# Narrow attention on four row strips, single-pass scores in the first and third wide attention, and a beginning in another order

## What is computed

```python
x = L0(ctx, x)   # attention of the tokens over (context, tokens), 16 heads of 16; MLP
x = L1(x, ctx)   # two wide cross-attentions (16 heads of 128, 64 keys + a bias key); MLP
x = L2(x, ctx)   # narrow cross-attention, 16 heads of 16, 64 keys, mask; MLP
x = L3(x, ctx)   # as L1
# wide:   weights = softmax((norm(x) @ wq + bq) . (ctx @ wk + bk, bias_k) / sqrt(128))
#         x += (weights @ (ctx @ wv + bv, bias_v)) @ wo + bo
# narrow: scores = where(mask, q . k * 16**-0.5, min);  x += softmax(scores) @ v @ cproj + b
# MLP:    x += gelu(norm(x) @ w1 + b1) @ w2 + b2
```

## Time and profile before

| | us |
|---|---|
| median of 3 runs | 928.24 (927.35 to 928.96) |
| profiled execution, its time | 924.61 |
| profiled execution, its span | 922.8 |
| PE busy | 859.1 (93%) |
| DVE busy | 630.1 (68%) |
| POOL busy | 550.4 (60%) |
| ACT busy | 496.9 (54%) |

### The profile page before, as it was taken

How to read it: one execution, slowest core, us unless ns; L and a number is a source line. 1 busy time by engine, 2 the same in 40 slices (tenths; PEclk the granted TensorE clock), 3 DMA queues, 4 the chain that set the end, 5 groups by cost and what they waited for, 6 DMA issues and landing times.

```text
span 922.8 us, 16592 instructions
## 1 busy us (share of the span) xinstructions
PE 859.1 (93%) x5936; PEld 711.8 (77%) x5936; DVE 630.1 (68%) x1329; ACT 496.9 (54%) x1204; POOL 550.4 (60%) x638
## 2 busy tenths in 40 slices
PE   4899977899999999999899898999999999999898
PEld 3677756899966799666798686899966699766798
DVE  3678886518889768897432499418889768898330
ACT  2677767555753357533563344755753357533562
POOL 2678884577943469564295053577853369564393
PEclk8899999999999999999999999999999999999999
DMA  6843212002550025200001100202550024100001
GB/s 192 278 125 104 92 40 104 1 1 92 163 215 1 1 69 171 104 1 1 6 19 36 57 1 1 104 1 87 165 217 1 1 69 161 46 1 1 1 13 35
DMA packets 26677, 64.09 MB, mean 69 GB/s; under 512 B 2995, under 2 KB 15843, under 8 KB 25444
## 3 DMA queue, kind: packets, MB, share of 16 engines
q1 hardware_dynamic: 26596, 63.03, 20.7%
HBM read 57.22 MB, written 5.77 MB: 68 GB/s over the span
## 4 chain that ended last, share of the span: by engine, by line
PE 67%; DVE 19%; POOL 4%; issue 4%; DMA 2%; ACT 2%; SPq 1%; DVEq 0%; POOLq 0%
PE ps L1008 7%; PE ps L948 6%; PE ps L909 6%; PE ps L937 5%; PE ps L984 5%; PE ps L734 3%; PE ps L735 3%; PE ps L736 3%; PE ps L715 3%; DVE prob L1699 3%; PE ps L791 3%; PE ps L716 3%; PE ps L717 3%; DVE mx L1698 3%; DVE z L1534 3%
## 5 line engine op out<-in xcount | busy, mean ns | idle before, releaser
L1008 PE MATMUL ps<-arena,pT_all 128*128 128x256 f32 x512 | 116.6, 381 | 5.9 <-DVE x L1719 3.8
L1008 PEld LDWEIGHTS ps<-arena,pT_all 128*128 128x128 f32 x512 | 96.2, 190 | 32.5 <-issue 15.3
L558 POOL TENSOR_TENSOR rstd<-var,neg_half 128x1 f32<-128x1 f32 (+1 forms) x56 | 33.9, 606 | 137.8 <-DVE var L1528 137.8
L984 PE MATMUL ps<-arena,hT 128*128 128x512 f32 x256 | 115.5, 594 | 0.0
L598 POOL TENSOR_TENSOR prob<-prob,rinv 128x512 f32<-128x512 f32 x32 | 49.5, 1548 | 108.7 <-DVE rinv L1712 108.7
L565 POOL TENSOR_TENSOR arena<-arena,rinv 128x640 f32<-128x640 f32 x64 | 80.4, 1258 | 42.1 <-DVE rinv L1513 41.7
L1280 ACT ACTIVATE arena_r<-ps,cols 128x256 fp32r<-128x256 f32 x128 | 66.5, 520 | 55.5 <-PE ps L717 55.3
L619 POOL TENSOR_TENSOR arena_r<-arena,arena_r 128x512 fp32r<-128x512 f32 x64 | 84.0, 1331 | 9.9 <-ACT arena L1281 9.9
L715 PE MATMUL ps<-hH,w1H 128*128 128x256 f32 x256 | 74.9, 293 | 11.9 <-DVE prob L1699 5.2
L1237 ACT ACTIVATE arena<-ps,nb 128x320 f32<-128x320 f32 x128 | 66.3, 524 | 33.5 <-DVE nb L1499 32.8
L1388 ACT ACTIVATE prob<-prob 128x512 f32<-128x512 f32 x32 | 20.2, 631 | 116.2 <-DVE prob L1699 116.2
(11 more groups left out here) (176 smaller groups left out, 2459.1 us busy)
## 6 DMA issues: line engine op xcount, KB each, us to landing
ring<-in_heads_dram SPq DMA_DIRECT2D x64, 512.5 KB, 3.4
w<-in_w_dram SPq DMA_DIRECT2D x8, 1024.0 KB, 8.0
first_r<-spare_k SPq DMA_DIRECT2D x24, 160.0 KB
first_q<-spare_q SPq DMA_DIRECT2D x48, 64.0 KB, 2.5
spare_k<-HL SPq DMA_DIRECT2D x8, 320.0 KB, 2.5
spare_q<-HL SPq DMA_DIRECT2D x8, 256.0 KB, 2.5
x<-in_x_dram SPq DMA_DIRECT2D x1, 1024.0 KB, 6.1
lnb<-in_lnb_dram SPq DMA_DIRECT2D x4, 256.0 KB, 6.8
```

The source lines that it names most:

```text
L984: last = mm(ps[:, SCORES[k][half], :], hT[:, k, d, 0:P], A[:, d, b // 2, cols_of, sl, :].rearrange("p r s k -> p r (s k)"), start=(d == 0) ...
L1008: last = mm(ps[:, 6, 0:D], pT[:, k, c, :], VW[:, b, c, :], start=(c == 0), stop=(c == PAIRS - 1))
```

## The change

What it does, by place:

- **Beginning.** `kinT` of batch 0 is loaded first, the two halves of `w0` apart, each with its own semaphore; the constants wait no longer for each other, the mask is made between the splits; `kinT` of batch 1 is loaded early, and `base(4)` and `base(5)` stand ahead of the first scores. PE multiplies `ones` by `ones` 7 times ahead of the first base and 4 times ahead of the first scores.
- **Attention 0 and 2.** `A` is kept as a high fp32r part (written by ACT) and a low one (`A_low`, DVE: psum minus high), the tile as `hH` and `hL` (DVE, `tile_low`). Scores are three fp32r matmuls in the place of one f32 matmul: high by high, high by low, low by high. ACT copies both halves of `VW`. DVE adds to `x` inside the softmax and no longer behind it; ACT copies the transposed weights between the two exponentials.
- **Loads.** `A_low` lies over the MLP's weights. So `load_mlp(1)` and `load_mlp(3)` go behind the fifth head of attention 1 and 3.
- **Narrow attention.** Keys are unpadded (two blocks), kept twice, with zeros for the heads of the other parity. Scores are 8 matmuls of 32 rows on four row strips into four banks; the mask comes in as 4 matmuls of one row per tile. The sums are taken for 16 heads in 128 columns, DVE inverts these, and 8 small matmuls (`inverses`) spread the inverses to the outputs' rows, which ACT copies. Queries: 4 matmuls, and ACT adds the bias. Values and output come one tile later. `project` has 6 jobs, stands ahead of the MLP's last addition but for its last job, and the first six tiles' variances are taken at the end of `mlp(1)`.

```diff
 # SP
+                    if a % 2 == 1 and h == RING:
+                        load_mlp(a)
...
             load_keys(0)
-            load_mlp(1)
             load_keys(1)
 # PE, beginning
+                pe.wait_ge(pool_set, 1)
+                keep_busy(7)
+                pe.wait_ge(in_base, 32)
                 for t in range(4):
                     base(t)
...
+                pe.wait_ge(in_kin1, 16)
+                pe.wait_ge(hl_ready, 1)
+                base(4)
                 pe.wait_ge(consts_ready, 1)
+                pe.wait_ge(hl_ready, 5)
+                base(5)
+                keep_busy(4)
 # PE, scores of the wide attention
+                    if a % 2 == 0:
+                        pe.wait_ge(h_low, TILES * (a // 2) + g + 1)
+                        passes = ((hH, A_high), (hH, A_low), (hL, A_high))
+                    else:
+                        passes = ((hT, A),)
...
                         for d in range(DH):
-                            last = mm(ps[:, SCORES[k][half], :], hT[:, k, d, 0:P],
-                                      A[:, d, b // 2, cols_of, sl, :].rearrange("p r s k -> p r (s k)"),
-                                      start=(d == 0), stop=(d == 1))
+                            for p, (hp, Ap) in enumerate(passes):
+                                last = mm(ps[:, SCORES[k][half], :], hp[:, k, d, 0:P],
+                                          Ap[:, d, b // 2, cols_of, sl, :].rearrange("p r s k -> p r (s k)"),
+                                          start=(d == 0 and p == 0), stop=(d == 1 and p == len(passes) - 1))
 # PE, scores and inverses of the narrow attention
-                    for m in range(4):
-                        for s in range(2):
-                            at = slice(C * s, C * s + C)
-                            last = mm(ps[:, s, m * P:(m + 1) * P], qT2[at, k, m, :], KC[at, m, b, :], start=True, stop=True)
+                    for j in range(4):
+                        at = slice(32 * j, 32 * j + 1)
+                        mm(ps[:, j, 0:D], ones_r[at, :], mask2[at, b * C:(b + 1) * C].unsqueeze(1).broadcast_to([1, 4, C]),
+                           start=True, stop=False)
+                    for m in range(DH):
+                        for j in range(4):
+                            at = slice(32 * j, 32 * j + 32)
+                            last = mm(ps[:, j, m * P:(m + 1) * P], qT2[at, k, m, :], KC[at, m, b, :],
+                                      start=False, stop=(m == 1))
...
+                def inverses(g):
+                    pe.wait_ge(inv2_ready, g + 1)
+                    for m in range(DH):
+                        for j in range(4):
+                            at = slice(32 * j, 32 * j + 32)
+                            last = mm(ps[at, 4, D + m * P:D + (m + 1) * P],
+                                      spread_of[at, m, :, :].rearrange("p e t -> p (e t)"), inv2[at, :], start=True, stop=True)
 # DVE, keys of attention 0 and 2
+                    if a % 2 == 0:
+                        slots = slice(0, 4, 3) if par == 0 else slice(1, 3)
+                        dve.wait_ge(a_act, n + 1)
+                        v.tensor_tensor(A_low[:, :, :, h // 2, slots, :].rearrange("p d g s k -> p (d g) s k"),
+                                        ps[:, 2 + k, :].rearrange("p (dg s k) -> p dg s k", dg=4, s=2),
+                                        A_high[:, :, :, h // 2, slots, :].rearrange("p d g s k -> p (d g) s k").bitcast(F32),
+                                        ALU.subtract).then_inc(a_low, 1)
+                        if h == 1:
+                            tile_low(a, 0)
+                            tile_low(a, 1)
+                        continue
 # DVE, tokens of attention 0 and 2
+                    if a % 2 == 0 and 1 <= g < TILES - 1:
+                        tile_low(a, g + 1)
...
+                    if g >= 2 and a % 2 == 0:
+                        add(g - 2)
 # ACT, keys of attention 0 and 2
+                        if a % 2 == 0:
+                            a_(VW[0:C, h % 2:B:2, h // 2, :], ps[0:C, 4 + k, :].rearrange("p (g n) -> p g n", g=2),
+                               ACT.Copy)
```

More of the change, by code:

```diff
@@ L820, in output, with keep_busy @@
                     last.then_inc(o_ps, 1)
+                def keep_busy(n):
+                    for i in range(n):
+                        mm(ps[:, 6, 0:P], ones[:, :], ones[:, :], start=True, stop=True)
                 def aside(step, b):
```

432 lines of the change are left out of this document (262 added, 170 removed).

## The result

The changed kernel takes 918.4 us (median of 4 runs, 917.06 to 922.0) where the kernel before, run beside it, takes 928.2: ratio 0.991 with an interval of 0.9885 to 0.9938. That is faster by 9.8 us, and less than half of the 24.6 that were forecast; it lies above the range of 893 to 916. The profiled executions, 924.6 and 918.1, differ by 6.5; the median moved 3.3 further, since the profiled execution of the kernel before was 3.6 under its median.

The account below looks back on a forecast made before the run. PE, busy 93% of the time, was taken to bound the kernel. 3.0 + 10.4 + 15.7 - 0.5 - 4.0 = 24.6 us gained: 900.0 for the profiled execution, 903.6 for the median, range 893 to 916.

Parts of the forecast that it names:

- Beginning: Start of the kernel: earlier loads and faster bases reach POOL's first addition sooner; 3.0 us gained, ends 1.4 and 4.5.
- Scores of attention 0 and 2: `tokens(0)` and `tokens(2)`: single-pass fp32r scores cut PE's tile to 7.26, DVE's becomes 7.4; 5.2 us each, 10.4 gained.
- the 0.42 that the sum takes off for the addition's leaving: DVE's tile in attention 0 and 2: 7.15 + 0.35 - 0.42 + 0.30 = 7.4, the addition leaving its end.
- The sum's 0.83 us of room per tile: `tokens(0)`: DVE has 0.83 us per tile left before it bounds, PE's tile 7.98 against DVE's 7.15.
- The fourth rival: DVE takes `tokens(0)` and `tokens(2)` whole, tile at 7.98, all 10.4 lost: 914.0 us, chance 0.08.
- Keys of attention 0 and 2: Keys stages: PE covers ACT's added copy and DVE's subtraction; 0.5 us lost for two starts, ends 0 and 19.
- the slower rival: ACT and DVE bound the keys of attention 0 and 2: 28.8 lost in place of 0.5, 931.9 us, chance 0.05.
- Weights in the ring's list: Attention 1 and 3: w1 and w2 ahead of the sixth head's load make it late; 2.0 us each, 4.0 lost.
- The first and second rivals: Ring in time and DVE hides: 898.6 us, chance 0.19; ring late by 5.1 in both: 909.8 us, chance 0.13.
- Narrow attention: Narrow attention: front 10.5, loop 3.5 and end 1.7 gained, together 15.7 us; ends 8 and 19.
- Loop: Narrow attention, first to eighth scores: 37.5 us against 41.0, tiles 5.9 where some 6.3; 3.5 gained.
- End: Narrow attention, eighth scores to last output: 18.4 us where it was 20.1; 1.7 gained.

Follow-up runs that it names:

- begin_nobusy: Changed kernel with POOL's first additions of x and brow five steps later and without the eleven multiplications of `ones`: 918.37 us.
- ring: Changed kernel with the second and fourth MLP's w1 and w2 loads issued ahead of the sixth head's wait for a ring place: 915.19 us, ratio 0.9868.
- low: Changed kernel with `tile_low` of the next tile moved behind z and the statistics in attention 0 and 2: 919.71 us.
- stats: On top of `low`, statistics come first behind DVE's multiplication, then z, then the low part, in attention 0 and 2: 914.33 us, ratio 0.9868.
- tail: Changed kernel with DVE's order altered at the narrow attention's end and the eighth output in its own bank: 918.98 us.
- fill_tail2: `all_fill` with the third pair of rows' statistics ahead of the narrow attention's last two additions: 898.16 us, ratio 0.9683.
- fill: Changed kernel with 13 multiplications of `ones` in PE's gaps around the first two narrow tiles: 918.15 us, ratio 0.9901.
- before_begin: Kernel before the change, with POOL's first additions five steps later and the split of ctx twelve steps later: 923.73 us.
- all: Changed kernel with `ring`, `stats`, `tail`, POOL's first additions later, and the narrow loop's products ahead of maxima, values ahead of queries: 902.89 us, ratio 0.9733.
- all_fill: `all` plus the 13 multiplications of `ones` of `fill`: 900.52 us, ratio 0.9707.

## Why the prediction was wrong, by its own steps

By the profiles 24.6 were forecast and 6.5 came. Of the 18 between them, 9.6 lie in the narrow attention behind its first scores, 3.4 in attention 0 and 2, 2.0 in the beginning, 1.5 in mlp(1), 1.1 in the keys of attention 0 and 2, and 0.7 in those of attention 1 and 3.

*Beginning, 3.0 forecast, 1.0 in the first profile and 0 in the second.* Two steps failed. The first is the up to 3.0 that the `ones` were to give back in the bases: these took 6.88 (6.93 before), and `begin_nobusy` leaves no gain that is shown. `brow` was then issued only 0.9 sooner (27.97 for 28.87), and it took 7.6 us to land as before, with POOL's due scalings behind it. In `ring`, where the bases took 4.21, `brow` was issued at 26.13 and the first addition came at 33.95, 2.6 sooner than in the kernel before: so far the way "through SP's list" held. The second step that failed is that this gain goes on to mlp(0). I had named this DMA as what sets the pace, and then counted the gain ahead of it in full; with the additions in their place the first `up` is 0.4 sooner on average over eight profiles, and 2.2 when they are moved in both (seven profiles against one). The lower end I gave (1.4, bytes alone) was nearest.

*Scores of attention 0 and 2, 10.4 forecast, 7.0.* PE's part was right (2.8 us of scores; 7.33 where PE bounds). The mis-sized term is DVE's tile: 7.4 forecast, 7.77 measured, 0.37 on most tiles of two attentions, and the first tile's transposes wait for POOL besides (1.38 for 0.37). The step that failed is the 0.42 that the sum takes off for the addition's leaving. The addition had stood where it covered POOL's multiplication, and DVE's tile was 7.15 with it and without it (the rows from 277.95 on); 7.15 + 0.35 + 0.30 is 7.80. `low` and `stats` show the wait. The sum's 0.83 us of room per tile wasn't there either in the first half of `tokens(0)`, where DVE's multiplications lay 7.15 apart as in `tokens(1)`. The fourth rival had the right place and three times the price (10.4 for 3.4).

*Keys of attention 0 and 2, 0.5 forecast, 1.6.* Small, in the first heads (one distance of 4.32); its cause was not looked for and stays open. Heads follow 3.15 apart, so the slower rival (ACT and DVE bound them) did not come.

*Weights in the ring's list, 4.0 forecast, 4.7.* Right, shown by `ring`. The first and second rivals (in time; late by 5.1) are out.

*Narrow attention, 15.7 forecast, 6.0: under the lower end of 8 that I gave.* Front: 10.5 forecast, 10.4. Loop: 3.5 gained forecast, 1.0 lost. Of the 4.5 between them 2.7 lie in the second and third distance (5.85 and 6.27, where I had 4.7 each: I left out ACT's table and copies in the second, and the values and inverses of the third), and 1.8 in the last four: three at 6.27 and one at 6.62 where I had 5.9. PE's list is 5.87 and not 5.45 (output 1.14 for 0.9, queries 1.06 for 0.9, inverses 0.58 for 0.45, transposes and z 1.3 for 1.15; scores and mask 0.77 for 1.1), its wait 0.40 where I had 0.45. End: 1.7 gained forecast, 3.4 lost (28.5 to 31.9; to the last output alone, as the forecast had it, 23.0 where it was 20.2 and 18.4 were forecast). The inverse takes a step of its own, so one tile more is in flight: behind the eighth scores stand four outputs, three values and three inverses, where before three outputs and two values stood: 1.04 + 1.02 + 3 x 0.57 = 3.8 us of PE that my layout of the list did not have. Of the waits there, `tail` and `fill_tail2` show DVE's order and the late statistics.

*What no step had: the clock.* The shorter work of the narrow attention leaves PE less busy at its start (4.42 us of 8.6 from 512.0 on in the first profile, which kept its clock; in the kernel before 6.83 of 8.6 from 522.3 on), and there the granted clock fell to 0.50 in nine of ten profiles without `fill`, at a cost of 2.2 to 3.3 us each in those with the unaltered loop, and in none of five with `fill`. In both profiles of the kernel before it was 1.00 from the first narrow scores to the eighth; they have 3.4 us at 0.50 just ahead of the first scores (519.6 to 523.0), where its queries take 3.36 us for 1.95. In mlp(1) of the changed kernel the clock fell behind a wait of 2.58:

```profile
444.00:447.40 3.40, 3.40 (x16) 3.40 (x17) 2.54 (x6) 3.38 (x7) 1.74 (x2) 0.51 0.02 5
```

That is the 1.47 of the table; the kernel before has the same wait, and its stage took 22.10 at full clock in its own profile and 23.59 in that of `before_begin`, so this piece is chance and not the change's.

## What to carry to other kernels

When an instruction is moved, ask what it was covering where it stood, not only what it costs where it goes: the addition took 0.33 us of DVE's list and shortened the next operation's wait for POOL by as much, so taking it away gained nothing. When the profile names a DMA as the pace of a stage, a gain ahead of it is mostly hidden until that DMA, or what waits for it, moves. And where a change makes PE's work shorter between waits, count the clock too: a few matmuls of `ones` in the gaps were worth 2.3 us here by the traces of `all` and `all_fill`.

## What was not expected of the hardware

Behind DVE's multiplication, two operations waited for POOL's (a subtraction with both operands in SBUF, 1.26 us for 0.42, and z, 1.13 for 0.41) and two did not (statistics 0.42, an addition that reads PSUM 0.42). POOL's multiplication of 512 columns takes 1.55 us and starts 0.05 behind DVE's, while its multiplication of 640 columns in the first attention takes 1.26 on average (L635 and L602 of the changed kernel's page), so it may be waiting for DVE's in turn; no run here tested that. The inverses, eight matmuls in four row strips that all write one PSUM bank, took 0.58 us together, where four column strips at once take 0.22; each strip writes its own 32 partitions. And PE's granted clock stood at 0.50 for 13.7 us behind gaps of only 0.59, 0.37 and 1.04 us, with work between them.
